# LN2 of the last group tile by tile, its neighbours' q, k, v behind the last product, and both stages in one block

## What is computed

```python
h = relu(layernorm(x))
h = h @ fc_in_w.T + fc_in_b                      # then 8 Euler steps of
f = alph * 0.5 * (adj @ h - h) + h @ w_eff - h + x0
h = h + f / 8
x = x + h
h = relu(layernorm(x))                           # LN2
q, k, v = h @ W                                  # 4 heads of 32
x = x + softmax(q @ k.T / sqrt(32) + mask(adj)) @ v
```

## Time and profile before

| | us |
|---|---|
| median of 3 runs | 691.7 (690.51 to 693.2) |
| the profiled execution | 692.22 |
| its span, first to last instruction | 690.4 |
| TensorE busy | 657.5 |
| VectorE busy | 483.6 |
| ScalarE busy | 399.4 |
| GpSimd busy | 121.3 |

### The profile page before, as it was taken

How to read it: one execution, slowest core, us unless ns; L and a number is a source line. 1 busy time by engine, 2 the same in 40 slices (tenths; PEclk the granted TensorE clock), 3 DMA queues, 4 the chain that set the end, 5 groups by cost and what they waited for, 6 DMA issues and landing times. The chain is left out here.

```text
span 690.4 us, 13190 instructions
## 1 busy us (share of the span) xinstructions
PE 657.5 (95%) x3801; PEld 512.6 (74%) x3801; DVE 483.6 (70%) x1336; ACT 399.4 (58%) x924; POOL 121.3 (18%) x100
## 2 busy tenths in 40 slices
PE   7999999999899998999999879999999999999996
PEld 5767997899788997889988766666666666666663
DVE  6663552377733777346543649999999999999993
ACT  3333232133541335422234268999999999999994
POOL 5010245012420124201132500000000000000001
PEclk9999999999999999999999888999999999999999
DMA  3101100311334103430044899777778777777720
GB/s 110 22 10 47 32 31 16 103 35 32 117 150 162 30 30 129 150 116 16 17 152 153 221 325 207 154 177 175 178 172 179 174 178 173 180 171 179 178 71 31
DMA packets 49808, 82.53 MB, mean 120 GB/s; under 512 B 5232, under 2 KB 13808, under 8 KB 49648
## 3 DMA queue, kind: packets, MB, share of 16 engines
q1 hardware_dynamic: 49344, 82.07, 45.0%
q10 hardware_dynamic: 432, 0.07, 0.1%
HBM read 52.76 MB, written 29.36 MB: 119 GB/s over the span
## 5 line engine op out<-in xcount | busy, mean ns | idle before, releaser
L1281 ACT ACTIVATE s_ring<-s_ring,low 128x512 f32<-128x512 f32 x256 | 182.5, 717 | 11.7 <-DVE low L1304 11.4
L1304 DVE CUSTOM_DVE_ANT_0 s_ring<-ps_s,pL 128x512 f32<-128x512 f32 x256 | 165.7, 685 | 18.5 <-PE ps_s L1344 17.9
L1331 PE MATMUL ps_t<-ident,s_ring 128*128 128x128 f32 x1024 | 156.0, 275 | 4.7 <-ACT p_t L1272 4.2
L1331 PEld LDWEIGHTS ps_t<-ident,s_ring 128*128 128x128 f32 x1024 | 124.0, 141 | 33.2 <-DVE p_t L1298 8.8
L1344 PE MATMUL ps_s<-pL,pH 128*128 128x512 f32 x256 | 124.8, 490 | 4.6 <-PEq L1400 3.4
L1298 DVE COPY p_t<-ps_t 128x512 f32<-128x512 f32 x128 | 85.0, 685 | 0.9 <-PE ps_t L1331 0.9
L1272 ACT ACTIVATE p_t<-ps_t 128x512 f32<-128x512 f32 x128 | 74.3, 582 | 0.3 <-PE ps_t L1331 0.3
L1344 PEld LDWEIGHTS ps_s<-pL,pH 128*128 128x128 f32 x256 | 49.3, 193 | 32.9 <-issue 16.4
L94 PE MATMUL ps_v<-rH,ut_h 128*128 128x384 f32 x192 | 65.1, 339 | 4.6 <-DVE v L927 4.6
L1258 POOL TENSOR_TENSOR o_n<-o_n,x 128x512 f32<-128x512 f32 x16 | 20.6, 1286 | 269.9 <-DVE o_n L1314 269.9
L1359 PE MATMUL ps_o<-p_t,v_sb 128*32 128x512 f32 x512 | 61.4, 598 | 3.7 <-ACT p_t L1272 3.0
(11 more groups left out here) (201 smaller groups left out, 1114.7 us busy)
## 6 DMA issues: line engine op xcount, KB each, us to landing
pH<-qk_dram SPq DMA_DIRECT2D x64, 256.0 KB, 6.9
pL<-qk_dram SPq DMA_DIRECT2D x64, 256.0 KB, 7.7
qk_dram<-qk SPq DMA_DIRECT2D x12, 512.0 KB, 3.3
x_ln<-in_x SPq DMA_DIRECT2D x16, 256.0 KB, 3.4
x_res<-in_x SPq DMA_DIRECT2D x16, 256.0 KB, 2.6
x_dram<-v SPq DMA_DIRECT2D x16, 256.0 KB, 3.1
v_sb<-v_dram SPq DMA_DIRECT2D x16, 256.0 KB, 9.4
x<-x_dram SPq DMA_DIRECT2D x16, 256.0 KB, 9.5
```

The lines of the kernel that those rows point to most:

```text
L1281: act.activation(s_ring[:, n % RING, :], s_ring[:, n % RING, :], ACT.Exp, bias=low[:, n:n + 1], scale=-1.0, accum_out=lsum[par][:, n:n + 1 ...
L1304: dve.tensor_tensor_reduce(s_ring[:, n % RING, :], ps_s[S_BANK[n]][:, :], mask[:, n // HEADS, :], -SCALE, 3.0e38, ALU.add, ALU.min, low[:, ...
L1331: mm = pe.transpose(ps_t[n % T_BANKS][:, j * 128:(j + 1) * 128], s_ring[:, n % RING, j * 128:(j + 1) * 128], ident[:, :])
```

## The change

One part joins the blocks: the stages become functions that return a program for each engine (`Programs`), and one block runs first the ODE and then the attention program on each. What the block end guarded is now single waits: `bank_free` (the first use of each PSUM bank), `saved` (ahead of SyncE's first loads) and `stored` (behind the first batch).

The other part is the last group. Items 2 to 9 of pair 1 of the group before leave its z and y steps; six of them (`EARLY`) and the four turns of h2, now by tile and into four banks at once, come first in the tail, the two others (`LATE`) inside `SEQ`. LN2 goes by tile: root, reciprocal, scale (GpSimd for tiles 0 to 2, VectorE for tile 3) and Relu within the y steps. Both `keep_warm` runs of the tail are gone. Four of the v evictions pass from ScalarE to VectorE (`tail_copy_v`). q and k of a batch are stored by one transfer each. The tail's results go to buffers of their own (`tail_slab`). `load_qk` of batch 0 and the load of adj are issued in y step 0, that of batch 1 behind the last y product. The layout of `v` changes from `[128, T, GB, 3 * D]` to `[128, 3, T, GB, D]` for all groups, so that two thirds of it can be the attention's `s_ring`.

The diff, cut to its core:

```diff
-WARM_START, WARM_NORM, WARM_END = 20, 48, 16
+WARM_START = 20
...
-    v = sb("v", [128, T, GB, 3 * D])
+    v = sb("v", [128, 3, T, GB, D])
+    keep["s_ring"] = v[:, 1:3, :, :, :].rearrange("p a t b d -> p (a t) (b d)")
...
+    REST = [i for i in range(NB) if BACK[i][0] != "t"]
+    REST_BANKS = [*ps_k, *ps_z]
+    EARLY, LATE = REST[:6], REST[6:]
+    SEQ = [("q", 0), ("k", 0), ("vt", 0), LATE[0], ("q", 1), LATE[1], ("k", 1), ("v", 0), ("vt", 1),
+           ("q", 2), ("k", 2), ("v", 1), ("vt", 2), ("q", 3), ("k", 3), ("v", 2), ("vt", 3), ("v", 3)]
+    SEQ_BANKS = [*ps_z, *ps_u, *ps_k]
+    HT_BANKS = [*ps_u, *ps_v]
...
+    keep["bank_free"] = [tail_freed(i) for i in (("k", 3), ("v", 2), ("t", 2), ("t", 3), ("vt", 2), ("q", 3), ("vt", 3), ("v", 3))]
+    keep["stored"] = [*((s, CREDIT + 16 * 2 * LAST) for s in qk_out), *((s, CREDIT + 32 * 2 * LAST) for s in qk1_out),
+                      (v_out, CREDIT + 16 * GB * LAST)]
+    keep["saved"] = [*keep["stored"], (x1_out, 16 * GB * LAST), (v_mm, T * B)]
...
-        back(1, 2, 8)
+        if not last:
+            back(1, 2, 8)
         for t in range(T):
             steps.y(g, t)
-            if t < 2:
+            if t < 2 and not last:
                 back(1, 8 + t, 9 + t)
...
+    def tail_scale(eng, t):
+        wait(eng, tail_rs, t + 1)
+        wait(eng, k_mm, NB * PR + 2)
+        for c in range(GB):
+            n = t * GB + c
+            ins = eng.tensor_scalar(h2[:, c, t, :], v[:, 0, t, c, :], mv_all[:, n, 0:1], std_all[:, n:n + 1],
+                                    ALU.subtract, ALU.mult)
+        ins.then_inc(tail_norm[t // (T - 1)], 1)
...
+        def y_step(g, t):
+            if not last_group(g):
+                return
+            if t == 0:
+                wait(sp, ln.u_mm, 3 * B)
+                wait(sp, ln.u0l_done, B)
+                sp.dma_start(ln.u0[:, :, :, :].rearrange("p b t d -> p b (t d)"),
+                             adj.rearrange("(p t) m -> p t m", t=T)).then_inc(keep["adj_in"], 16)
+                for s, done in zip((*qk_out, *qk1_out), (16, 16, 32, 32)):
+                    wait(sp, s, CREDIT + done * 2 * (LAST - 1))
+                load_qk(sp, qk_dram, keep, 0, 0)
+            if t == T - 1:
+                wait(sp, y_mm, T * NG)
+                load_qk(sp, qk_dram, keep, 1, 1)
...
+        def y_step(g, t):
+            if last_group(g) and t:
+                tail_scale(pool, t - 1)
...
+        def y_step(g, t):
+            if last_group(g):
+                if 1 < t < T:
+                    tail_relu(t - 2)
+                if t < T - 1:
+                    tail_root(t)
...
+            high(EARLY[0])
+            high(EARLY[1])
+            rest_vt(EARLY[2])
+            tail_relu(T - 2)
+            tail_root(T - 1)
+            high(EARLY[3])
+            tail_relu(T - 1)
+            high(("t", 0))
+            high(EARLY[4])
+            high(("t", 1))
+            rest_vt(EARLY[5])
+            high(("q", 0))
             act.activation(exp_out[:, :], ln2n.eps[:, 0:1], ACT.Exp).then_inc(exp_ready, 1)
+            high(("k", 0))
+            rest_v(LATE[0])
+            tail_vt(0)
+            high(("q", 1))
+            rest_v(LATE[1])
+            high(("k", 1))
+            high(("t", 2))
+            tail_vt(1)
+            high(("q", 2))
+            high(("k", 2))
+            high(("t", 3))
+            tail_vt(2)
+            high(("q", 3))
+            high(("k", 3))
+            tail_vt(3)
...
+            tail_recip(T - 1)
+            tail_scale(dve, T - 1)
+            low(EARLY[0])
+            low(EARLY[1])
+            low(("t", 0))
+            low(EARLY[3])
+            low(EARLY[4])
+            low(("t", 1))
+            low(("q", 0))
+            low(("k", 0))
+            low(("q", 1))
+            low(("k", 1))
+            tail_copy_v(0)
+            low(("t", 2))
+            low(("q", 2))
+            low(("k", 2))
+            tail_copy_v(1)
+            low(("t", 3))
+            low(("q", 3))
+            low(("k", 3))
+            tail_copy_v(2)
+            tail_copy_v(3)
...
-            keep_warm(pe, ps_v[0], ident, WARM_NORM)
-            keep_warm(pe, ps_v[0], ident, WARM_END)
...
+            rest(EARLY[0])
+            rest(EARLY[1])
+            turn(0)
+            turn(1)
+            rest(EARLY[2])
+            rest(EARLY[3])
+            turn(2)
+            turn(3)
+            rest(EARLY[4])
+            rest(EARLY[5])
+            for item in SEQ:
+                seq(item)
...
+            ode_ctx = kept.enter_context(ExitStack())
+            ode = ode_stage(nc, ode_ctx, sem, x, adj, x1_dram, qk_dram, v_dram, keep, ln)
         with ExitStack() as ctx:
-            attention_block(nc, ctx, x1_dram, qk_dram, v_dram, out, keep)
+            attention = attention_stage(nc, ctx, sem, x1_dram, qk_dram, v_dram, out, keep)
+            block = ctx.enter_context(nc.Block())
+            @block.sync
+            def _(sp):
+                ode.sync(sp)
+                attention.sync(sp)
+            @block.gpsimd
+            def _(pool):
+                ode.gpsimd(pool)
+                attention.gpsimd(pool)
...
```

More of the change, by code:

```diff
@@ L612, in tail_v, with tail_bank, tail_slab, tail_out_of @@
+    def tail_bank(item):
+        if item in SEQ:
+            return SEQ_BANKS[SEQ.index(item) % len(SEQ_BANKS)]
+        return HT_BANKS[item[1]] if item in HIGHS and item not in EARLY else REST_BANKS[REST.index(item) % len(REST_BANKS)]
+    def tail_slab(c):
+        if c < 2:
+            return ut[:, 4 * c:4 * c + 4, :]
+        return (z_h, z_l)[c - 2][:, :, :, :].rearrange("p t b d -> p t (b d)")
     def tail_v(c):
         return h2[:, c, :, :].rearrange("p t d -> p (t d)")
+    def tail_out_of(item):
+        if item in EARLY:
+            kind, c = BACK[item]
+            return qk_parts(kind, 1, c)
+        kind, c = item
+        if kind == "t":
+            return [ht_h[c % 2][:, :], ht_l[c % 2][:, :]]
+        row = 2 * ("q", "k").index(kind)
+        return [tail_slab(c)[:, row + part, :] for part in range(2)]
@@ L622, in back @@
                 steps.back(g - 1, pair, lo, hi)
+        last = not following
         steps.u(g, 0, prev)
@@ L721, in _, with gpsimd @@
             sp.sem_inc(s, CREDIT)
[L722 to L728, removed]
+        run(sp, Steps(u=u_step, v=v_step, y=y_step, back=back, tail=tail))
+    def gpsimd(pool):
         def v_step(g, b, following):
@@ L756, in tail, with scalar @@
                                    0.0, NEG, ALU.is_equal, ALU.mult).then_inc(keep["mask_done"], 1)
-        run(pool, Steps(v=v_step, z=z_step, tail=tail))
-    @block.scalar
-    def _(act):
+        run(pool, Steps(v=v_step, z=z_step, y=y_step, tail=tail))
+    def scalar(act):
         def u_step(g, b, prev):
@@ L855, in back, with vector @@
                     act.activation(v_nat[:, :], src, ACT.Copy).then_inc(vn_done, 1)
-        run(act, Steps(u=u_step, v=v_step, back=back, z=z_step, tail=tail))
-    @block.vector
-    def _(dve):
+        run(act, Steps(u=u_step, v=v_step, back=back, z=z_step, y=y_step, tail=tail))
+    def vector(dve):
         def x1_rows(b):
-            return lambda t: v[:, t, b, 0:D]
+            return lambda t: v[:, 0, t, b, :]
         def u_step(g, b, prev):
@@ L1091, in tail, with turn @@
-            wait(pe, *tail_count(TAIL_BANKS.index(ps_v[0]) + len(TAIL_BANKS)))
-            keep_warm(pe, ps_v[0], ident, WARM_END)
+            def turn(t):
+                if t == 0:
+                    for i in (VT[1], SPLIT[-1]):
+                        wait(pe, *freed(i, PR - 1))
+                    wait(pe, v_add, T * B)
+                wait(pe, h2_done, GB * LAST + t + 1)
+                for c in range(GB):
+                    pe.transpose(HT_BANKS[c][:, t * 128:(t + 1) * 128], h2[:, c, t, :], ident[:, :]).then_inc(tr_mm, 1)
@@ new lines, in make, with turn_v @@
+            def make(item, kind, c, high, low):
+                ps = tail_bank(item)
+                at = {"q": 0, "k": D, "vt": 2 * D}[kind]
+                split3(pe, ps[:, :], [((keep["wH"][:, at:at + D], keep["wL"][:, at:at + D]),
+                                       (high[:, :], low[:, :]))]).then_inc(k_mm, 1)
+            def turn_v(item, src):
+                for t in range(T):
+                    mm = pe.transpose(tail_bank(item)[:, t * 128:(t + 1) * 128], src[:, t * 128:(t + 1) * 128], ident[:, :])
+                mm.then_inc(k_mm, 1)
@@ L1167, in attention_block, with run @@
     o_out = [sem(f"o_out{i}") for i in range(2)]
-    def run(eng, batch, tail, tail_stores=False):
+    def run(eng, batch, tail, overlay=False):
         batch(0, 0)
-        if tail_stores:
-            wait(eng, tail_out, TAIL_STORED)
+        if overlay:
+            for s, value in keep["stored"]:
+                wait(eng, s, value)
         with eng.Fori(0, (B - 2) // LOOP_BATCHES) as turn:
@@ L1342, in batch @@
                         wait(pe, qk_in[par], parity_count(b, par, 128))
```

(2 more changed lines are left out.)

359 lines of the change are left out of this document (205 added, 154 removed).

## The result

The changed kernel took **687.1 us** (median of 7 runs, 685.7 to 688.7); the kernel before took 693.2 beside it (690.5 to 693.9). The ratio is 0.9927, 95% interval 0.9905 to 0.9949: faster, by 0.5 to 1% (3.5 to 6.6 us). The forecast was 684.4 in a range of 680.5 to 689.0, a ratio of 0.989 to the 691.7 it was made against. The direction and the range held; the gain was put 1 to 2 us too high. The profiled execution took 685.8 (span 684.0), against 692.2 before. In the slower state of the chip there was one execution in all, of the kernel before (920 us, granted clock 0.65); it is in no figure here.

The account below looks back on a forecast made before the run. TensorE, busy 657.5 of 690.4 us, was taken as the bound, with gain only where it waits or runs slow. 6.5 + 0.8 = 7.3 us off 692.2 gave 684.9, less 0.5 for the median: 684.4, range 680.5 to 689.0.

Parts of the forecast that it names:

- Step 1: Last group's products: with eight items moved behind them, the last product ends at 380.1 us, 4.7 us earlier.
- Step 2: Last product to first score: 17.1 us of TensorE work plus waits, ending at 405.5 us before any clock cost.
- step 3: Clock in the wait for LN2: one fall near 388 for 6 us, costing 2.1 us; first score at 407.6.
- the books: Tally of four engines' queues behind the last product, in the diff's order with earlier spacings; gave 406.4, corrected to 405.5.
- B: Rival: clock falls in every wait and stays low to the handover; first score at 413, 690.6 us, no change; chance 0.07.
- Step 4: First to sixteenth score behind the handover: 0.8 us come back with the clock up there, 0 without.
- E: Rival: something at the handover (mask, loads, a store) still holds an engine until 412; 690 us; chance 0.06.
- C: Rival: fixed orders in the tail bite more, four waits each 1 us longer; 688.4 us, half of it 686.4; chance 0.15.
- A: Rival: clock stays up through the wait; first score at 405.5, 682.3 us, or 681.4 with short scales; chance 0.22.

Follow-up runs that it names:

- the join: Changed kernel with one wait added: TensorE's first score waits until SyncE has gone through its whole part of the ODE stage; 691.6 us, ratio 0.9983.
- the evictions moved: Changed kernel with tile 3's root, the table load and two Relus reordered, and batches 2 and 3's turned-h2 high and low parts evicted earlier; 681.1 us, ratio 0.9825.

## Why the prediction was nearly right

- **Step 1 held.** The products end 4.5 us earlier (380.39 against 384.85; forecast 4.7).
- **Step 2 held as a sum, not term by term.** From there to the first score the trace has 27.46 us, the forecast, with step 3's 2.1 us for the clock, 27.5. But the waits were 0.45 + 1.04 + 1.94 + 1.75 + 1.56 + 0.78 = 7.5 us instead of 8.5. The remaining 2.8 us on top of the 17.1 us of work are hand-overs inside it and the slow clock, where the forecast had 1.9. That these errors cancel to within 0.1 us is luck, since two traces of the same code already differ by 0.6.
- **The step that failed is one sentence of step 2**: that hardly anything hangs on GpSimd's scales. I bounded four of them by 1.3 and 2.5 us; they took 3.1 (9.35 / 12 = 0.78 us each), above the upper bound, perhaps because the rows stood for one long operation and these are four short ones. So tile 2 was ready at 385.25, not 383.3. ScalarE's root for tile 3 stood behind the Relu that waits for it and started 1.3 us later than in the books: 0.42 us in that wait, 0.45 in the turn that waited for tile 1's scales, 0.3 because the products ended later, the rest in hand-overs. VectorE's scales took 1.49 us, not 2.0, and the reciprocal 0.18 instead of 0.31, which hid about half of the error in the forecast of the last turn (388.54; forecast 388.0). With the root moved the last turn came 1.5 us earlier.
- **Step 3: the fall came, once, but mis-sized.** It began at 390, not 388, and lasted 3.4 us, not 6; it cost 1 to 1.5 us in the trace, not 2.1, and nothing that the timed runs show. The handover had the full clock, as forecast, against B.
- The Trainium skill, "TensorE: Matmul & The Clock Gate", Part 4, has transposes not counting for the clock. Both runs speak against it here: 24 of them kept the clock at 1.00 where it had fallen in three executions without them, and without the 48 of before it fell 3.4 us earlier. The first rests on one profiled execution with them, the second on one of either kernel.
- **Step 4 held**: sixteen scores in 12.3 us (forecast 12.4, before 13.2). The strips of v cost nothing: one add in the loop took 556 ns before and after.
- **What the sum left out**: 0.5 us of the 7.1 is given back between the sixteenth score and the last batch's loads, and 0.2 more by the end. It is spread over the batches, some 0.04 us each: from the loads of batch 3 to those of batch 15 it takes 199.2 to 199.3 us in the changed kernel and in the runs with the join and with the evictions moved, 198.7 and 198.8 in the kernel before with and without its idle transposes. What takes it was not tested. The profiled execution thus gained 6.4 us against 7.3 forecast; the timed runs 3.5 to 6.6.
- **Rivals.** E is refuted by the first score at 407.85 and by the experiment with the join, which shows what E would have been: nearly no change. C is refuted too, although its 686.4 to 688.4 hold the median: it wanted waits longer than the books', and they were 1.0 us shorter, with the first score where the forecast had it. What it shares with the forecast is shown: each of the two waits ahead of q was an order written out by hand, and taking them away gave 3.3 us, more than any other change of order. A's condition, the clock up through the wait, was made by the 24 transposes: 687.3 us, no change that can be timed.

## What to carry to other kernels

Where two stages are joined, the gain here was the wait of the fast engine for the slow one at the seam, plus the clock that it loses meanwhile (3.15 and 0.85 us); find it in the timeline as the first instruction behind the seam and who released it. In an order written out by hand, look at each instruction with a long wait and ask what stands behind it on its engine that was ready: here moving a root, a table load, two Relus and the high and low parts of the turned h2 of two batches gave 6 us, more than half of it by the last. And bound a group of short operations by rows of short operations, since four of 128x128 took GpSimd longer than one of 128x512.

## What the chip showed that I had not expected

- GpSimd's scale of 128x128 with two operands per partition takes 0.78 us, four 3.1 us; a mask tile of 128x512 takes 2.43 us. VectorE's same scale took 0.37 us in the changed kernel (1.49 / 4), with the mask running beside it, where before single ones had reached 1.20.
- The granted clock fell at different places of the ODE stage in executions with the same code there, and add 3 lay between 380.59 and 384.10 us. Of the timed runs of the changed kernel, those with a mean granted clock of 0.989 or more took 685.7 us, those near 0.985 took 686.9 to 688.7. A difference of 2 us between the spans of two single profiles is therefore no evidence.
